# Combine turns of a two-layer token tower: vector operations of different rows laced, and head outputs in two row blocks in place of three

## The chip, the cores and the metric

The kernel runs on one core of a Trainium2 chip, in float32. The metric is the device time of one execution in microseconds (us). The kernel before was timed three times; its median is 1458.46 us.

A core has TensorE (PE in the profile; its weight loads are PEld), VectorE (DVE), ScalarE (ACT), GpSimd (POOL) and SyncE (SP, which here only issues transfers). Each engine takes its own instructions in the order in which they are written. Between engines, and between two instructions of one engine where one needs what the other writes, order is kept by semaphores.

## The reference, cut to what matters

The tower embeds 32 batches of 128 tokens with 192 features and runs two layers. Layer 0 is causal attention and a soft mixture of 64 experts. Layer 1 is attention with 12 heads of 16 features and a router that sends each token to one of 8 experts. The change lies in the stretch from the end of layer 0's experts up to layer 1's router:

```python
Y = einsum('bsd,bms->bmd', Ys, C)            # combine: softmax weights times slot outputs
h = h + Y
x = layernorm(h);  q, k, v = x @ w_qkv.T     # 12 heads of 16
q = rope(q * scale);  k = rope(k)
attn = softmax(q @ k.T)                      # per head, 128 x 128
h = h + (attn @ v) @ w_proj.T + b_proj
x = layernorm(h);  logits = x @ router_w
expert = argmax(logits)                      # row of the token: count of earlier tokens of this expert
```

## The kernel before, in words

`tower_program` has four phases one behind the other: `tower_phase` (embedding, attention 0, slot inputs), `expert_phase` for 64 experts, `combine_phase`, and `expert_phase` for 8 experts. Everything changed is in `combine_phase` and in the host layout of one weight.

`combine_phase` works on one batch of 128 tokens after the other, in 38 turns (t = 0 to 37). A turn works at up to eight stages of different batches at once. The letters of `turn(t, u, n, y, q, a, p, r, z, w)` name the batch that a stage handles: n (t+1) subtracts the maximum from the combine logits (`less_max`) and exponentiates them; y (t) makes Y = C·Ys, adds it to h, and normalises it to `x4`; q (t-1) makes q, k, v, rotates q and k, and transposes them; a (t-2) makes scores, softmax and head outputs; p (t-3) projects the heads and adds to h, and normalises it to `x5`. Of router pairs of two batches, r (odd turns from 5 on) makes logits, z (even turns from 6 on) chooses experts and counts, and w (odd turns from 7 on) works out the rows and scatters the tokens.

Each engine has a `turn` of its own in which the stages' operations are written out by hand in one order; that order is the schedule. The order of PE in a turn is: Y (8 matmuls), q and k (5), the projection (3), the router's transposes (r) or the counts (z), transposes of the probabilities (12), of q and k (6), router (r), of x4 (2), v (5), scores (12), transposes of the inverse sums (3), head outputs (12).

On DVE a turn begins with two reductions (L1709) that give the maximum of each head's scores; ACT then makes the exponentials (L1601), and PE's counts, router transposes and transposes of the probabilities wait for them. DVE goes on with `place` (w) or `choose` (z), `oT`, `less_max`, the addition of Y, the statistics of layer norm 4 (L1730 to L1733), the rotation (L1744 to L1753, ending in `qk_padded`), `x4` (L1759, L1760), statistics of layer norm 5 and the inverse sums. A dependent operation waits for a count in the semaphore `steps` (`st.link`, `st.wait`). At the end it waits for ACT's `x4T_hi` (L1628), which can start once v is made, and writes `x4T_lo` (L1781), `x4T_hi_over_lo` (L1783) and `x5` (L1789).

POOL makes both reciprocal square roots of a turn (L1428). In turns with w they are queued behind two indirect transfers that scatter the tokens (L1437), which wait for `to_i` (L1702).

The head outputs come out transposed. With 4 heads on 32 partitions each (16 in use), 12 heads take three row blocks of 128 columns, `bank[32*s:32*s+32, 1, g*P:(g+1)*P]` for head 4g+s. `oT` is these times the inverse sums; the sums are widened to 3×128 columns (L1774), transposed by PE (L1570) and copied by ACT (L1634). The projection adds three products with `Wproj_padded`, whose spare rows are zero but for the one of the bias.

## Time and profile before

| | us |
|---|---|
| runs shown | 1458.09, 1458.46, 1460.61 |
| median | 1458.46 |
| the profiled execution's own time | 1450.89 |
| its span in the profile | 1449.2 |

The profiled execution is 7.6 us shorter than the median of the runs shown. Times of single operations are read from it. Its mean granted TensorE clock is 0.979 of full speed. The combine turns run from about 914 us to about 1294 us of the span.

How to read it: a row of the timeline gives start, duration, engine, line, operation, written tile <- read tiles, shapes and count, and in brackets the idle time of the engine before it with what ended it. L60 is the helper `matmuls`, so its rows are told apart by their tiles. Durations of neighbouring DVE rows overlap by some 0.08 us where the second does not wait for the first.

### The profile page before, as it was taken

How to read it: one execution, taken by the hardware profiler on the slowest of the kernel's cores; microseconds unless marked ns; L12 is line 12 of the kernel's file. 1: busy time of each engine (PE TensorE's matmuls, PEld its weight loads, DVE VectorE, ACT ScalarE, POOL GpSimd, SP SyncE). 2: the span in 40 equal slices, each digit the busy share in tenths (PEclk: the TensorE clock that was granted, in tenths of full speed). 3: DMA queues.
4: the chain of work that ended last, by engine and by line, in shares of the span. 5: the costliest groups of instructions: out<-in, count | busy, mean ns of one | idle time of the engine just before them, and what ended most of it. 6: DMA issues, size and time to landing. Idle time of an engine off the chain costs nothing. (4 is left out here: it accounts for less than half of the span.)

```text
span 1449.2 us, 29984 instructions
## 1 busy us (share of the span) xinstructions
PE 1364.3 (94%) x9221; PEld 1214.8 (84%) x9221; DVE 1002.1 (69%) x2920; ACT 940.8 (65%) x2207; POOL 261.1 (18%) x284
## 2 busy tenths in 40 slices
PE   6899999988899999999999999799999999869995
PEld 4678888877799989999899998689999899758885
DVE  7787777543777777777777774489989899832321
ACT  1378888876566666666666664288888888725551
POOL 6231100000111111111111110102122122121344
PEclk8899999999999999999999999999999999979998
DMA  7036666567466666666666665545445447116641
GB/s 214 20 110 161 161 150 150 150 165 193 141 184 198 188 192 196 183 198 188 192 196 183 198 188 167 159 139 155 133 154 153 130 146 198 42 41 148 145 79 19
DMA packets 202709, 221.17 MB, mean 153 GB/s; under 512 B 30068, under 2 KB 169402, under 8 KB 202608
## 3 DMA queue, kind: packets, MB, share of 16 engines
q1 hardware_dynamic: 170032, 180.15, 44.9%
q10 hardware_dynamic: 24896, 32.80, 6.7%
q0 software_dynamic: 7680, 6.95, 2.6%
q8 instruction: 54, 0.88, 0.3%
q14 instruction: 47, 0.39, 0.1%
HBM read 142.46 MB, written 79.90 MB: 153 GB/s over the span
## 5 line engine op out<-in xcount | busy, mean ns | idle before, releaser
L1116 PE MATMUL bank<-e_w,e_h_full 128*128 128x192 f32 x1920 | 324.5, 326 | 0.3
L1116 PEld LDWEIGHTS bank<-e_w,e_h_full 128*128 128x128 f32 x1920 | 310.6, 190 | 1.2 <-ACT e_h_full L1187 0.8
L1187 ACT ACTIVATE e_h_full<-bank,e_b 128x512 f32<-128x512 f32 x240 | 165.1, 688 | 193.6 <-PE bank L60 193.6
L1053 POOL TENSOR_TENSOR e_ln_rstd<-e_ln_var_eps,minus_half 128x4 f32<-128x4 f32 x64 | 64.8, 1013 | 515.1 <-DVE e_ln_var_eps L1238 515.1
L1601 ACT ACTIVATE probs<-bank,head_neg_max 128x128 f32<-128x128 f32 x384 | 134.5, 392 | 2.5 <-DVE head_neg_max L1709 1.2
L1245 DVE TENSOR_SCALAR e_rows<-e_slot_sums,e_ln_mean_var,e_ln_rstd 128x192 f32<-128x192 f32 x256 | 80.0, 377 | 76.2 <-POOL e_ln_rstd L1053 76.2
L1157 ACT ACTIVATE e_x_full<-bank,e_ln_shift,e_ln_gain 128x512 f32<-128x512 f32 x128 | 92.5, 773 | 48.7 <-PE bank L1089 44.9
L885 PE MATMUL bank<-x,dispatch_weights 128*128 128x193 f32 x512 | 95.8, 330 | 11.0 <-ACT slot_stage L739 10.4
L60 PE MATMUL bank<-e_x_hi,e_w1hi 128*128 128x512 f32 x216 | 95.6, 443 | 4.6 <-DVE e_w1lo L1224 3.0
L621 DVE TENSOR_REDUCE column_neg_max<-bank 128x4 f32<-128x512 f32 x64 | 44.2, 690 | 80.5 <-PE bank L60 80.3
L1483 PE MATMUL bank<-slot_outputs_then_w_part,combineT 128*128 128x193 f32 x512 | 94.2, 337 | 2.7 <-ACT combineT L1593 2.1
L1270 DVE TENSOR_TENSOR e_stage<-bank,e_b 128x768 f32<-128x768 f32 x64 | 61.3, 958 | 48.3 <-PE bank L1116 48.3
L885 PEld LDWEIGHTS bank<-x,dispatch_weights 128*128 128x128 f32 x512 | 82.1, 190 | 14.3 <-issue 14.3
L1483 PEld LDWEIGHTS bank<-slot_outputs_then_w_part,combineT 128*128 128x128 f32 x512 | 84.7, 192 | 9.2 <-issue 9.2
L1601 ACT ACTIVATION_READ_ACCUMULATOR probs<-bank,head_neg_max 128x1 f32 x384 | 89.1, 232 | 0.0
L60 PE MATMUL bank<-e_x_hi,e_w1lo 128*128 128x512 f32 x216 | 85.3, 395 | 0.0
L60 PE MATMUL bank<-e_x_lo,e_w1hi 128*128 128x512 f32 x216 | 85.2, 394 | 0.0
L60 PE MATMUL bank<-e_x_hi_over_lo,e_w1hi 128*128 128x512 f32 x216 | 84.9, 393 | 0.0
L60 PE MATMUL bank<-e_x_hi_over_lo,e_w1lo 128*128 128x512 f32 x216 | 84.6, 392 | 0.0
L67 PE MATMUL bank<-spare_operand 128*128 128x512 f32 x253 | 69.0, 421 | 14.2 <-PEq L1383 8.6
L719 ACT ACTIVATE slot_exp<-bank,column_neg_max 128x128 f32<-128x128 f32 x256 | 72.8, 374 | 14.6 <-DVE column_neg_max L621 14.6
L1163 ACT ACTIVATE e_x_hi<-e_x_full 128x1024 fp32r<-128x1024 f32 x72 | 76.2, 1058 | 7.6
(255 smaller groups left out, 3138.1 us busy)
## 6 DMA issues: line engine op xcount, KB each, us to landing
slot_sums<-slot_stage SPq DMA_DIRECT2D x64, 386.0 KB
e_slot_sums<-slot_sums SPq DMA_DIRECT2D x64, 386.0 KB, 3.6
slot_outputs<-e_stage ACTq DMA_DIRECT2D x64, 384.0 KB, 3.3
slot_outputs_then_w_part<-slot_outputs SPq DMA_DIRECT2D x32, 768.0 KB, 4.9
e_w<-in_w SPq DMA_DIRECT2D x64, 288.0 KB, 2.9
slot_logits<-kept_logits SPq DMA_DIRECT2D x64, 256.0 KB, 3.3
slot_logits<-slot_logits SPq DMA_DIRECT2D x32, 512.0 KB, 3.4
e_w1raw<-in_w SPq DMA_DIRECT2D x80, 192.0 KB, 2.8
```

Source lines behind the costliest of these rows:

```text
L60: last = pe.matmul(out, w, m, start=n == 0, stop=n == len(pairs) - 1, **kw)
L67: pe.matmul(out, T["spare"][:, 0:P], T["spare"][:], start=True, stop=True)
L719: last = act.activation(ls[:, n % 2, js], logits_bank(n)[:, js], ACT.Exp, bias=nmc[:, n % 2, j:j + 1])
L885: last = pe.matmul(U[:, j // 2, j % 2, :], disp[:, n % 2, j * P:(j + 1) * P], x3[n // NC % 3][:, j, 0:1 + D], start=True, stop=True)
L1053: pool.tensor_tensor(rs[u][:], ve[u][:], half[:], ALU.pow).then_inc(rstd_ready, 1)
L1116: last = pe.matmul(ybank(u)[:, j // 2, (j % 2) * D:(j % 2 + 1) * D], hf[:, k, js], w2s[u][:, k, :], start=k == 0, stop=k == MT - 1)
L1157: last = act.activation(xf[:, k, :], bank[:, k, :], ACT.Identity, bias=lnb[:, k, ds(n, 1)], scale=lng[:, k, ds(n, 1)])
L1163: act.activation(xhi[u][:], xf[:], ACT.Copy).then_inc(x_hi_ready, 1)
L1187: act.activation(hf[:, m, :], hbank(u, m), act_fn, bias=b1s[:, m, ds(n, 1)]).then_inc(acted, 1)
L1245: last = dve.tensor_scalar(rows[u][:, j, 0:D], sums[u][:, j, 1:], mv[u][:, j, 0:1], rs[u][:, j:j + 1], ALU.subtract, ALU.mult)
L1483: last = pe.matmul(bank[:, 0, 0:D + 1], cT[:, c, :], ysb[u][:, c, :], start=c == 0, stop=c == NC - 1)
L1601: last = act.activation(pr[:, s, g, :], bank[:, 4 + s, g * P:(g + 1) * P], ACT.Exp, bias=nmx[:, s, g:g + 1], accum_out=esum[:, s, g:g + 1])
```

## The change

It has two parts.

**Head outputs.** Heads 2k and 2k+1 of the first eight share the 32 partitions of group k: v is stored by head with 32 columns, an even head's 16 features in the first half and an odd head's in the second half, the other half zero. Two products into the same partitions and columns are added up. The first eight heads thus fill one row block, and the last four take a second one. There are still 12 head matmuls. The transposes of the inverse sums go from 3 to 2, the projection's products from 3 to 2, `oT` and `einvT` from 384 to 256 columns. The sums are widened in two copies of 128 columns in place of one of 384. The bias row moves to row 16 of the second part.

**Order on DVE.** `choose` and `place` are dissolved, and their dependent operations, those of the layer norms and the reciprocals are written between operations of other stages. The waits remain, but for a count noted by `mark` when the earlier operation was issued. The diff, cut to its core:

```diff
+    def mark(self, ins):
+        self.did(ins)
+        return self.base + self.n
...
-        einv_wide, oT = sb("head_inv_wide", [P, 3, 4, 2 * HD]), sb("oT", [P, 3 * P])
-        einvT = sb("head_invT", [P, 3 * P])
+        einv_wide, oT = sb("head_inv_wide", [P, 2, P]), sb("oT", [P, 2 * P])
+        einvT = sb("head_invT", [P, 2 * P])
...
-                        matmuls(pe, projected, [(oT[:, g * P:(g + 1) * P], Wp[:, g, :]) for g in range(3)]
+                        matmuls(pe, projected, [(oT[:, g * P:(g + 1) * P], Wp[:, g, :]) for g in range(2)]
...
-                        for g in range(3):
-                            for s in range(4):
-                                last = pe.matmul(bank[32 * s:32 * s + 32, 1, g * P:(g + 1) * P], vs[u][:, 4 * g + s, :],
-                                                 pT[:, s, g, :], start=True, stop=True)
+                        for first, step, rows, start, stop in ((0, 2, 0, True, False), (1, 2, 0, False, True),
+                                                               (8, 1, 1, True, True)):
+                            for k in range(4):
+                                head = first + step * k
+                                last = pe.matmul(bank[32 * k:32 * k + 32, 1, rows * P:(rows + 1) * P], vs[u][:, head, :],
+                                                 pT[:, head % 4, head // 4, :], start=start, stop=stop)
...
-                        act.activation(vs[1 - u][:, :, 0:HD], bank[:, 3, 0:D].rearrange("p (a d) -> p a d", d=HD),
+                        by_halves = vs[1 - u][:].rearrange("p (i b) (e d) -> p i (b e) d", b=2, e=2)
+                        act.activation(by_halves[:, :, 0:4:3, :],
...
                     if w is not None:
-                        place(w)
+                        part = st.mark(dve.tensor_reduce(lsum[:], lex[:], AX_X, ALU.add))
...
                     if n is not None:
                         less_max(n)
+                    if w is not None:
+                        st.wait()
+                        dve.tensor_copy(to_i[w % 3][:], row_f[:]).then_inc(S["placed"], 1)
...
                         st.did(dve.tensor_tensor(straight[:], src, cos[:], ALU.mult))
+                    if y is not None:
+                        wait_apart(dve, S["h2_ready"], y + 1)
+                        stats4 = st.mark(dve.bn_stats(st6[:, 0, :], h[:, y, :]))
...
+                    if a is not None:
+                        dve.wait_ge(S["S_exp"], 4 * a + 4)
+                        inverse = st.mark(dve.reciprocal(einv[:], esum[:]))
+                    if p is not None:
+                        wait_apart(dve, S["h3_ready"], p + 1)
+                        stats5 = st.mark(dve.bn_stats(st6[:, 1, :], h[:, p, :]))
                     if y is not None:
                         dve.wait_ge(S["ln4_rstd"], y + 1)
```

What this makes of the order is seen in three places. The first is DVE in an odd turn with w, from the operation behind the two reductions to the first one of the rotation. `to_i` is the row number that starts POOL's scatter, `row_inv` and `h_all` add Y, and BN_STATS and BN_AGGR are layer norm 4. Before:

```order
L1695 TENSOR_TENSOR row_by_expert<-row_by_expert,onehot 128x16
L1697 TENSOR_REDUCE router_sum<-router_exp 128x2
L1699 TENSOR_REDUCE row_of_token<-row_by_expert 128x2
L1700 RECIPROCAL x_rows<-router_sum 128x2
L1702 CAST to_i<-row_of_token 128x2
L1721 TENSOR_TENSOR oT<-bank,head_invT 128x384
L1660 TENSOR_TENSOR slot_logits<-slot_logits,token_neg_max_rows 128x1024
L1726 RECIPROCAL row_inv<-bank 128x1
L1727 SCALAR_TENSOR_TENSOR h_all<-bank,row_inv,h_all 128x192
L1730 BN_STATS ln_stats<-h_all 128x6
L1732 BN_AGGR ln_mean_var<-ln_stats 128x2
L1733 TENSOR_SCALAR ln_var_eps<-ln_mean_var 128x1
```

After:

```order
L1705 TENSOR_TENSOR row_by_expert<-row_by_expert,onehot 128x16
L1707 TENSOR_REDUCE router_sum<-router_exp 128x2
L1717 TENSOR_TENSOR oT<-bank,head_invT 128x256
L1720 TENSOR_REDUCE row_of_token<-row_by_expert 128x2
L1721 RECIPROCAL x_rows<-router_sum 128x2
L1666 TENSOR_TENSOR slot_logits<-slot_logits,token_neg_max_rows 128x1024
L1729 CAST to_i<-row_of_token 128x2
L1736 RECIPROCAL row_inv<-bank 128x1
L1743 SCALAR_TENSOR_TENSOR h_all<-bank,row_inv,h_all 128x192
L1755 TENSOR_TENSOR rope_straight<-bank,rope_cos 128x384
L1758 BN_STATS ln_stats<-h_all 128x6
L1760 TENSOR_TENSOR rope_crossed<-bank,rope_sin 128x192
```

`oT` and `less_max` (L1666) now stand ahead of the cast `to_i`, and the statistics of layer norm 4 stand inside the rotation.

The second place is DVE in the same turn, from `qk_padded`, for which PE's transposes of q and k wait, to the router's maximum. The tile x is `x4`, for which PE's two transposes ahead of v wait. Before:

```order
L1753 TENSOR_TENSOR qk_padded<-rope_straight,rope_crossed 128x24x16
L1759 TENSOR_SCALAR x<-h_all,ln_mean_var,ln_rstd 128x192
L1760 TENSOR_SCALAR x<-h_all,ln_mean_var,ln_rstd 128x64
L1766 BN_STATS ln_stats<-h_all 128x6
L1768 BN_AGGR ln_mean_var<-ln_stats 128x2
L1769 TENSOR_SCALAR ln_var_eps<-ln_mean_var 128x1
L1773 RECIPROCAL head_inv<-head_exp_sum 128x12
L1774 COPY head_inv_wide<-head_inv 128x384
```

After:

```order
L1775 TENSOR_TENSOR qk_padded<-rope_straight,rope_crossed 128x24x16
L1780 RECIPROCAL head_inv<-head_exp_sum 128x12
L1783 BN_STATS ln_stats<-h_all 128x6
L1787 TENSOR_SCALAR x<-h_all,ln_mean_var,ln_rstd 128x192
L1788 TENSOR_SCALAR x<-h_all,ln_mean_var,ln_rstd 128x64
L1792 BN_AGGR ln_mean_var<-ln_stats 128x2
L1688 COPY head_inv_wide<-head_inv 128x128
L1691 COPY head_inv_wide<-head_inv 128x128
L1799 TENSOR_SCALAR ln_var_eps<-ln_mean_var 128x1
```

A reciprocal and the statistics of layer norm 5 now stand between `qk_padded` and `x4`.

The third place is PE, from the transposes of the inverse sums of one turn into the next. Before:

```order
L1570 MATMUL bank<-ident,head_inv_wide 128x128 x3
L1581 MATMUL bank<-probsT,v_padded 32x128 x12
L1483 MATMUL bank<-e_slot_outputs_then_w_part,combineT 128x193 x8
L60 MATMUL bank<-Wqkv_hi,x4T_hi 128x384
L60 MATMUL bank<-Wqkv_lo,x4T_hi 128x384
L60 MATMUL bank<-Wqkv_hi,x4T_lo 128x384
L60 MATMUL bank<-Wqkv_hi,x4T_hi_over_lo 128x384
L60 MATMUL bank<-Wqkv_lo,x4T_hi_over_lo 128x384
L60 MATMUL bank<-Wproj_padded,oT 128x192 x3
```

After:

```order
L1574 MATMUL bank<-ident,head_inv_wide 128x128 x2
L1586 MATMUL bank<-probsT,v_by_head 32x128 x12
L1487 MATMUL bank<-e_slot_outputs_then_w_part,combineT 128x193 x8
L60 MATMUL bank<-Wqkv_hi,x4T_hi 128x384
L60 MATMUL bank<-Wqkv_lo,x4T_hi 128x384
L60 MATMUL bank<-Wqkv_hi,x4T_lo 128x384
L60 MATMUL bank<-Wqkv_hi,x4T_hi_over_lo 128x384
L60 MATMUL bank<-Wqkv_lo,x4T_hi_over_lo 128x384
L60 MATMUL bank<-Wproj_two_parts,oT 128x192 x2
```

Nothing moved on PE; one transpose and one product of the projection are gone from each turn.

## Rows read from the trace of the kernel before

**Rows 1.** Windows: busy us of each engine, granted clock, DMA, in 22 turns

```profile
963.74:1201.00 237.26, 234.96 (x2448) 215.77 (x2450) 214.59 (x678) 197.80 (x726) 52.88 (x75) 1.00 0.48 145
```

**Rows 2.** Timeline: the first DVE reduction of turns 5, 21, 22, 23 and 32

```profile
963.55 0.95 DVE L1709 TENSOR_REDUCE head_neg_max<-bank 128x6 f32<-128x768 f32 x1
...
1136.32 0.95 DVE L1709 TENSOR_REDUCE head_neg_max<-bank 128x6 f32<-128x768 f32 x1
...
1147.44 1.81 DVE L1709 TENSOR_REDUCE head_neg_max<-bank 128x6 f32<-128x768 f32 x2
...
1157.79 1.81 DVE L1709 TENSOR_REDUCE head_neg_max<-bank 128x6 f32<-128x768 f32 x2
...
1254.71 0.95 DVE L1709 TENSOR_REDUCE head_neg_max<-bank 128x6 f32<-128x768 f32 x1
```

**Rows 3.** Timeline of even turn 22: PE, ACT and DVE behind the exponentials

```profile
1152.77 0.30 PEld L60 LDWEIGHTS bank<-onehot,upto 128*128 128x128 f32 x2
...
1154.82 0.64 PEld L1528 LDWEIGHTS bank<-ident,qk_padded 128*128 128x128 f32 x6 [0.27 <-DVE qk_padded L1753]
...
1155.43 0.25 PEld L1546 LDWEIGHTS bank<-ident,x 128*128 128x128 f32 x2
...
1156.55 0.38 ACT L1628 ACTIVATE x4T_hi<-bank 128x256 fp32r<-128x256 f32 x1
...
1157.05 0.28 DVE L1781 TENSOR_TENSOR x4T_lo<-bank,x4T_hi 128x128 fp32r<-128x128 f32 x1
```

**Rows 4.** Timeline of odd turn 21: PE and ACT behind the exponentials

```profile
1141.66 0.42 PEld L1505 LDWEIGHTS bank<-ident,x_rows 128*128 128x128 f32 x4
...
1143.65 0.64 PEld L1528 LDWEIGHTS bank<-ident,qk_padded 128*128 128x128 f32 x6 [0.26 <-DVE qk_padded L1753]
...
1145.15 0.25 PEld L1546 LDWEIGHTS bank<-ident,x 128*128 128x128 f32 x2
...
1146.27 0.38 ACT L1628 ACTIVATE x4T_hi<-bank 128x256 fp32r<-128x256 f32 x1 [0.90 <-PE bank L60]
```

**Rows 5.** Timeline of turn 21: small DVE operations, the last one waiting for `row_of_token`

```profile
1138.33 0.17 DVE L1699 TENSOR_REDUCE row_of_token<-row_by_expert 128x2 f32<-128x16 f32 x1
...
1138.42 0.15 DVE L1700 RECIPROCAL x_rows<-router_sum 128x2 f32<-128x2 f32 x1
...
1138.61 0.17 DVE L1702 CAST to_i<-row_of_token 128x2 int32<-128x2 f32 x1
```

**Rows 6.** Timeline of turn 22: head matmuls, last product of q and k, DVE's rotation

```profile
1147.46 0.59 PEld L1581 LDWEIGHTS bank<-probsT,v_padded 128*32 128x32 f32 x24 [0.17 <-issue]
...
1151.69 0.34 PE L60 MATMUL bank<-Wqkv_lo,x4T_hi_over_lo 128*128 128x384 f32 x1
...
1152.21 0.36 DVE L1730 BATCH_NORM_STATS2 ln_stats<-h_all 128x6 f32<-128x192 f32 x1
...
1152.97 0.55 DVE L1744 TENSOR_TENSOR rope_straight<-bank,rope_cos 128x384 f32<-128x384 f32 x1
...
1154.22 0.55 DVE L1753 TENSOR_TENSOR qk_padded<-rope_straight,rope_crossed 128x384 f32<-128x384 f32 x1
...
1154.98 0.31 DVE L1760 TENSOR_SCALAR x<-h_all,ln_mean_var,ln_rstd 128x64 f32<-128x64 f32 x1
```

**Rows 7.** Timeline of turn 21: DVE's `less_max`, POOL's scatter; last the scatter of turn 31

```profile
1139.19 1.22 DVE L1660 TENSOR_TENSOR slot_logits<-slot_logits,token_neg_max_rows 128x1024 f32<-128x1024 f32 x1
...
1139.58 1.74 POOL L1437 DMA_INDIRECT routed_inputs<-x_rows,to_i  x1 [3.93 <-DVE to_i L1702]
...
1141.62 0.98 POOL L1437 DMA_INDIRECT routed_inputs<-x_rows,to_i  x1 [0.30 <-issue]
...
1142.61 0.59 POOL L1428 TENSOR_TENSOR ln_rstd<-ln_var_eps,minus_half 128x1 f32<-128x1 f32 x1
...
1246.93 1.04 POOL L1437 DMA_INDIRECT routed_inputs<-x_rows,to_i  x1 [3.90 <-DVE to_i L1702]
```

**Rows 8.** Groups by line: loads of the projection's weights, 6 in each of 32 turns

```profile
L60 PEld LDWEIGHTS bank<-Wproj_padded,oT 128*128 128x128 f32 x192 | 32.3, 189 | 3.7 <-DVE oT L1721 3.6
```

More of the change, by code:

```diff
@@ L246, in __init__ @@
         self.C_ready, self.C_exp = sem("C_ready"), sem("C_exp")
[L247 removed]
+        self.Wp = sb("Wproj_two_parts", [P, 2, D])
     def load_logits(self, sp, b):
@@ L1568, in turn @@
                         pe.wait_ge(S["einv_ready"], a + 1)
[L1569 to L1571 removed]
+                        for g in range(2):
+                            last = pe.transpose(bank[:, 2, g * P:(g + 1) * P], einv_wide[:, g, :], ident[:])
                         last.then_inc(S["einvT_done"], 1)
@@ L1750, in turn @@
                     if q is not None:
-                        st.wait()
+                        dve.wait_ge(steps, turned)
                         past(dve, S["qkT_done"], q)
@@ L1838, in host_layout, with projection_parts @@
     }
-def padded_projection(w, b):
-    t = np.zeros((4, 2 * HD, 3, D), np.float32)
-    t[:, 0:HD] = w.reshape(3, 4, HD, D).transpose(1, 2, 0, 3)
-    t[0, HD, 0] = b
-    return t.reshape(P, 3, D)
+def projection_parts(w, b):
+    t = np.zeros((2, P, D), np.float32)
+    t[0] = w[0:P]
+    for k in range(4):
+        first = 2 * HD * k + HD * (k % 2)
+        t[1, first:first + HD] = w[P + HD * k:P + HD * (k + 1)]
+    t[1, HD] = b
+    return np.ascontiguousarray(t.transpose(1, 0, 2))
 def rope_tables():
```

104 lines of the change are left out of this document (55 added, 49 removed).

## The prediction

> **What bounds the kernel now.** I read four views. The windows come first, for whether one engine is simply full. In 22 turns of 237.26 us PE is busy for 234.96, DVE for 214.59 and ACT for 197.80, at full clock (2.4 GHz, granted 1.00) [rows 1]. That looks like PE, but a matmul's row runs on while it waits in the pipe, so the second view is the start of each turn. The two reductions of DVE begin at 1136.32, 1147.44 and 1157.79: 11.12 us for an odd turn, 10.35 for an even one; from turn 5 to turn 32 it is 291.16 us for 14 odd and 13 even turns [rows 2]. 14 × 11.12 + 13 × 10.35 is 290.2; 0.9 us are small irregular pauses.
>
> The third view, the timeline, shows a ring through three engines that closes once a turn. I count from the start R of the reductions. ACT turns the maxima into 12 exponentials, and PE may go on with counts or router transposes at R + 5.33 (even, 1152.77) or R + 5.34 (odd, 1141.66) [rows 2 to 4]. PE then transposes the probabilities and reaches the transposes of q and k, where it waits 0.27 and 0.26 us for DVE's `qk_padded` [rows 3, 4]. Behind it come the transposes of x4, v, ACT's `x4T_hi` (1.12 us behind the first x4 transpose in both turns), DVE's `x4T_lo` and, two operations on, the next R: 0.74 us from 1157.05 to 1157.79 [rows 2 to 4]. So the reader is to see a ring with one stall in it of some 0.27 us a turn, and in the even turn another 0.08, since `x4T_lo` starts 0.12 behind the end of `x4T_hi` (1156.93) where 0.04 is a release.
>
> **The change part by part.**
>
> *Less work on PE.* A weight load of the projection takes 0.168 us per issue (32.3 us / 192), and two of the six of a turn go: 0.33 us [rows 8]. A transpose is about 0.12 us (two x4 transposes, 0.25) [rows 3]: 0.12 us for the one that goes. But both lie ahead of the point at which PE waits for the exponentials, and the projection is no part of the ring. PE merely comes to that point 0.45 us sooner and waits. Worth to the ring: nothing directly. The transpose lets everything from the head outputs to the product of q and k start 0.12 us sooner.
>
> *Head matmuls.* They stay 12. Before, 24 loads take from 1147.46 to about 1148.2, and the row says 0.59 [rows 6]. The new thing is that four of them add to what the four before have written. The trace has no such pair in this size; bounds are 0 and, if the second four waited until the first four are through, about a third of 0.59 for a pause, 0.2 us. I take 0, since each product here is already two passes into one place (24 loads for 12 products).
>
> *Less copying.* `oT` and the transposed sums have 256 columns in place of 384. On DVE 384 columns take 0.55 us and 192 features 0.36 [rows 6], so 128 columns less are some 0.13 us. The widening becomes two copies of 128, about as long together as the one, and it has cover: what waits for it is PE's third-to-last step of the turn. ACT's shorter copy has cover too.
>
> *Lacing.* The row of small operations gives its price: an operation that needn't wait starts 0.09 us behind the other (1138.33 to 1138.42), one that waits for it 0.19 (to 1138.61) [rows 5]. So a link costs 0.1. From R to the rotation's first operation it is 5.53 us now (1152.97) [rows 2, 6]. The statistics that move behind that operation are 0.76 of it (1152.21 to 1152.97) [rows 6], links 0.3, `oT` 0.13: DVE could start at R + 4.3. But the rotation reads PE's product of q and k, whose last matmul ends at 1152.03, R + 4.59 [rows 6]; 0.12 sooner and with a release of 0.05 it is R + 4.52. PE ends last there now. From the rotation's start to `qk_padded` it is 1.25 us now (to 1154.22) [rows 6], and with the statistics in it (0.36, then two small ones, each less the overlap of 0.08) 0.48 more. So `qk_padded` starts at R + 6.25 in place of R + 6.78, and is through for PE at R + 6.85. PE is there at 1154.55, R + 7.11 [rows 3]. **The stall goes**, with 0.26 us to spare. In odd turns the product comes up to 0.2 later after R, and PE reaches the place at R + 7.07: it goes too, with little to spare.
>
> *What is late next, even turns.* The operations on x4 now stand behind a reciprocal and BN_STATS. Now the second ends at 1155.29, 1.07 us behind the start of `qk_padded` [rows 6]; added are 0.15 for the reciprocal [rows 5] and 0.28 for the statistics (0.36 less 0.08) [rows 6], and 0.04 for the release: PE may start its x4 transposes at R + 6.25 + 1.54 = R + 7.79. Without any stall it would be there at 1155.43 − 0.27, R + 7.72; now it is there at R + 7.99 [rows 2, 3]. The ring gains 0.20 of the 0.27, and DVE is no longer late for `x4T_lo`, since the widening stands further ahead: 0.08. **Even: 0.27 us** (between 0.1 and 0.35).
>
> *What is late next, odd turns.* The router's matmuls stand between, so PE comes to the x4 transposes at 1145.15 − 0.26, R + 8.57 [rows 2, 4]; DVE alone would be ready by R + 8. But x4 needs the reciprocal square root that POOL makes behind the two scatter transfers [rows 7]. They wait for the cast `to_i`, at R + 2.29 now [rows 2, 5]. It moves behind `oT` and `less_max` (start to start some 0.34 + 1.13) less 0.2 for links: R + 3.55, 1.25 later. The first transfer thus starts at R + 4.5 (1139.58 + 1.25). How long is it? 1.74 us where `less_max` runs beside it, 1.04 where it doesn't [rows 7]; after the change `less_max` is over by then. I take 1.04, then the pause of 0.30, 0.98 for the second, up to 0.46 more since `qk_padded` (also two operands in SBUF) now runs beside it, and 0.59 for the square root: R + 7.9. Then the two operations on x4 and releases, 0.65: R + 8.55. PE would be there at R + 8.57. So it just fits. **Odd: 0.26 us**; if the transfer stays 1.74 it is nothing (below).
>
> The Trainium skill, page "SBUF — State Buffer", section "SBUF: two separate sides", says that a Vector operation with two SBUF inputs and a GpSimd operation that reads SBUF share a port pair that one of them holds for its whole instruction. The trace agrees in that the transfer is 0.70 us longer beside `less_max` [rows 7]; by the rule the moved transfer would be the short one.
>
> *Placements without cost.* `chosen` and the counts come later, with PE's wait for the exponentials as cover. SP's queue isn't touched; the projection's weight is a third smaller and is loaded long before. ACT's order is unchanged.
>
> **The sum.** 14 × 0.26 + 13 × 0.27 = 7.2 us. The turns before 5 and after 31 have the same steps with less to hide them; the last batch's own chain loses 0.33 + 0.12 once, and two full turns without router may gain 0.1 each: 0.6. Together 7.8 us. Against the profiled execution's 1450.89 that is 1443.1; that execution was 7.6 us below the median of the runs shown, and I carry the difference over: 1458.5 − 7.8 = 1450.7 us. The irregular 0.9 us I leave; with the stall gone some may be hidden.
>
> **The rivals.**
>
> *The scatter stays long.* If the first transfer takes 1.74 at its new place, the square root is there at R + 4.5 + 1.74 + 0.30 + 0.98 + 0.59 = R + 8.1 or more and x4 at R + 8.8. That is where PE starts today (1145.15, R + 8.83): the 13 odd turns with a scatter gain nothing, 3.4 us less, 1454.1. For it: the new place has other DVE operations beside it, `qk_padded` and the statistics among them; against it: the 1.04 of turn 31.
>
> *Links cost nothing.* If laced operations don't start sooner, only `oT`'s 0.13 is left. `qk_padded` comes 0.13 sooner, odd turns gain 0.13, and in even turns x4 is through at R + 6.65 + 1.54 = R + 8.19, 0.20 later than now, less the 0.08: 14 × 0.13 − 13 × 0.12 is 0.3; with the 0.6 it is some 1457.6. Against it are the 0.09 and 0.19 [rows 5].
>
> The Trainium skill, page "VectorE: DVE Perf Modes", section "The DRAIN you can't avoid", says just this: that a semaphore between two operations costs nothing extra, since the next one waits for an empty pipe anyway. By it the change would give the time of this rival; the rows above disagree with it for small operations.
>
> *Slower: the odd turn hangs on POOL.* If both transfers take 1.74 at the new place, the square root is ready at R + 4.5 + 1.74 + 0.30 + 1.74 + 0.59 = R + 8.9 and x4 at R + 9.55, 0.72 later than now. 13 × 0.72 is 9.4 us lost, less 3.5 of the even turns and 0.8 of the rest: about 5 us slower, 1463.6. It decides from the point at which the square root comes later than R + 8.2. For it: the cast is moved 1.25 us, and nothing on POOL was taken away. Against: the second transfer, beside the rotation, takes 0.98 today.
>
> *Slower: added-up head outputs pause.* 0.2 us ahead of Y and of q and k in each turn; `qk_padded` is then through at R + 7.05 in even turns (no stall) but x4 at R + 7.99, and in odd turns a stall of 0.15 returns: only some 3 us are left of the gain, 1455.5. This is the near end of that unknown; it takes a pause above 0.4 to be slower.
>
> *More than that.* If DVE is quicker than I counted, even turns save 0.35, and the pauses of 0.9 are covered: 9.9 us, 1448.6. More is not to be had, since the ring without stalls is R + 10.86 and R + 10.0, whatever DVE does.
>
> **How the numbers follow.** Forecast, with the better case, 0.55. Scatter long or a pause in the head outputs, still faster: 0.21. Links cost nothing: 0.10. Slower by POOL, or by something of its kind: 0.14. The predicted time is 1450.7 us. The range runs from 1447 (more than the better case by the spread of the runs, 1.5 us) to 1458 (the case without gain); left out are the slower case and a little below. 0.2% of the time, 2.9 us, is about what a measurement of this kernel can tell from no change. Faster by more is the first two, 0.76; within is the third, 0.10; slower is the last, 0.14.
>
> **What the profile after would show.** No idle time of PE ahead of the transposes of q and k, and instead idle time ahead of the counts and router transposes, ended by ACT's exponentials, of some 0.5 us a turn. R to R of 10.86 and 10.08 us. In even turns at most 0.1 us ahead of the x4 transposes, ended by DVE's x4. The first scatter of a pair at R + 4.5 with 1.04 us. PE's busy share falls although the time does. Wrong would be: idle time ahead of the x4 transposes of odd turns ended by DVE, with POOL's square root behind R + 8.2 (the scatter), a start of the rotation behind R + 4.7 (head outputs or DVE), or a turn that shortens by more than 0.35 us, which would mean that the exponentials' part of the ring isn't fixed.

## The result, and the profile after

The changed kernel takes 1447.94 us, the median of six runs (1443.63 to 1450.16). The kernel before takes 1457.32 us beside it, also of six (1452.49 to 1460.61). The ratio is 0.9944, with a 95% interval of 0.9921 to 0.9966: faster, by 3.4 to 7.9 parts in a thousand. Timed again later (experiment 11) the ratio was 0.9956 [0.9937, 0.9975]. The forecast was 1450.7 us.

The profiled execution of the changed kernel took 1449.45 us, with a span of 1447.7. That is only 1.4 us less than the profiled one of before, although the medians lie 9.4 apart. Where the turns run, the gain is seen in full. These are the same stages as in [rows 1], 22 turns, in the windows' view (us, then busy us of PE, PE's loads, DVE, ACT and POOL, the granted clock, DMA share, GB/s):

```profile
969.05:1199.40 230.35, 225.95 (x2380) 205.67 (x2371) 193.04 (x700) 193.13 (x726) 46.09 (x75) 1.00 0.49 150
```

The start R of DVE's reductions in turns 5, 21, 22, 23 and 32 of the changed kernel (timeline: start, duration; compare [rows 2]):

```profile
968.86 0.95 DVE L1699 TENSOR_REDUCE head_neg_max<-bank 128x6 f32<-128x768 f32 x1
...
1136.53 1.82 DVE L1699 TENSOR_REDUCE head_neg_max<-bank 128x6 f32<-128x768 f32 x2
...
1147.40 1.81 DVE L1699 TENSOR_REDUCE head_neg_max<-bank 128x6 f32<-128x768 f32 x2
...
1157.43 1.82 DVE L1699 TENSOR_REDUCE head_neg_max<-bank 128x6 f32<-128x768 f32 x2
...
1251.90 0.95 DVE L1699 TENSOR_REDUCE head_neg_max<-bank 128x6 f32<-128x768 f32 x1
```

The 27 full turns from 5 to 32 take 283.04 us, where they took 291.16 [rows 2]: 8.12 less. An odd turn takes 10.87, an even one 10.03 us.

The two spans are balanced by four stretches. (1) The first reduction of turn 2 stands at 933.62 before and at 939.37 after. The phases ahead of it, which the change doesn't touch, took 5.75 us more in this execution:

```profile
939.37 1.81 DVE L1699 TENSOR_REDUCE head_neg_max<-bank 128x6 f32<-128x768 f32 x2
```

(2) Turns 2 to 4 take 0.44 us less. (3) The 27 full turns take 8.12 less. (4) From turn 32 on, the last rows up to the end of the last scatter take 39.44 in place of 38.48 us, 0.96 more, and what is behind them 0.39 more. 5.75 − 0.44 − 8.12 + 0.96 + 0.39 = −1.46, the difference of the spans. In the twelve other profiled executions of this study the same point came between 937.5 and 944.7 us; the one of before is the early one.

How the ring looks now is seen in even turn 22, R = 1147.40 (timeline of the changed kernel; the brackets give the idle time ahead and what ended it, and are printed from 0.15 us on):

```profile
1151.90 0.56 DVE L1755 TENSOR_TENSOR rope_straight<-bank,rope_cos 128x384 f32<-128x384 f32 x1 [0.25 <-PE bank L60]
...
1152.73 0.30 PEld L60 LDWEIGHTS bank<-onehot,upto 128*128 128x128 f32 x2 [0.51 <-ACT probs L1606]
...
1153.56 0.55 DVE L1775 TENSOR_TENSOR qk_padded<-rope_straight,rope_crossed 128x384 f32<-128x384 f32 x1
...
1154.48 0.69 PEld L1532 LDWEIGHTS bank<-ident,qk_padded 128*128 128x128 f32 x6
...
1154.65 0.31 DVE L1788 TENSOR_SCALAR x<-h_all,ln_mean_var,ln_rstd 128x64 f32<-128x64 f32 x1
...
1155.14 0.25 PEld L1550 LDWEIGHTS bank<-ident,x 128*128 128x128 f32 x2
```

The stall of [rows 3] ahead of the transposes of q and k is gone: no bracket at 1154.48. None stands ahead of the x4 transposes (1155.14) either. PE's pause has moved ahead of the counts, 0.51 us, and it is ACT's last exponential that ends it. The odd turn 21, R = 1136.53, with POOL:

```profile
1138.42 0.42 DVE L1717 TENSOR_TENSOR oT<-bank,head_invT 128x256 f32<-128x256 f32 x1
...
1138.90 1.21 DVE L1666 TENSOR_TENSOR slot_logits<-slot_logits,token_neg_max_rows 128x1024 f32<-128x1024 f32 x1
...
1140.99 1.04 POOL L1441 DMA_INDIRECT routed_inputs<-x_rows,to_i  x1 [6.04 <-DVE to_i L1729]
...
1141.86 0.42 PEld L1509 LDWEIGHTS bank<-ident,x_rows 128*128 128x128 f32 x4 [0.28 <-ACT probs L1606]
...
1142.33 0.98 POOL L1441 DMA_INDIRECT routed_inputs<-x_rows,to_i  x1 [0.30 <-issue]
...
1142.92 0.55 DVE L1775 TENSOR_TENSOR qk_padded<-rope_straight,rope_crossed 128x384 f32<-128x384 f32 x1
1143.32 0.59 POOL L1432 TENSOR_TENSOR ln_rstd<-ln_var_eps,minus_half 128x1 f32<-128x1 f32 x1
...
1144.23 0.31 DVE L1788 TENSOR_SCALAR x<-h_all,ln_mean_var,ln_rstd 128x64 f32<-128x64 f32 x1
...
1145.11 0.25 PEld L1550 LDWEIGHTS bank<-ident,x 128*128 128x128 f32 x2
```

The first scatter is 1.04 us long in place of 1.74 [rows 7], and x4 is there at 1144.54, 0.57 us before PE takes it. The waits of 24 turns say the same (engine and line, for whom it waited, us in total, times, longest):

```profile
PEld bank L60 <- ACT probs L1606: 6.3, 12, 0.8
...
PEld bank L1509 <- ACT probs L1606: 3.2, 11, 0.3
```

These two are the waits for the exponentials in even and in odd turns. Before, the same view of the same stretch has 14 waits of PE for `qk_padded`, 11 of them in even turns and three in odd ones (9, 15 and 21), and hardly one for ACT's exponentials:

```profile
PEld bank L1528 <- DVE qk_padded L1753: 3.6, 14, 0.3
...
PEld bank L60 <- ACT probs L1601: 0.3, 1, 0.3
...
PEld bank L1505 <- ACT probs L1601: 0.2, 1, 0.2
```

### The profile page after: what moved, and what is told of

It is laid out like the page before. It is cut to its first block and busy times, and to the rows that moved or that the text cites. A ratio compares the mean times of both kernels' runs of the same rounds, so it can differ in the third digit from the quotient of the medians.

```text
span 1447.7 us, 29824 instructions
## 1 busy us (share of the span) xinstructions
PE 1357.5 (94%) x9125; PEld 1204.7 (83%) x9125; DVE 972.3 (67%) x2952; ACT 935.1 (65%) x2207; POOL 253.5 (18%) x284
```

## The experiments

Twelve kernels were run. The table gives, from the profiled execution of each, the 27 full turns, the median odd and even turn, the time from R of turn 32 to the end of the last scatter ("drain"), and the span; then the time, and the ratio to the kernel before on the same chip where it was timed in rounds.

| | 27 turns | odd | even | drain | span | time (median) | ratio |
|---|---|---|---|---|---|---|---|
| before | 291.16 | 11.12 | 10.35 | 38.48 | 1449.2 | 1457.32 | 1 |
| changed | 283.04 | 10.87 | 10.03 | 39.44 | 1447.7 | 1447.94 | 0.9944 |
| 1 heads only | 286.37 | 10.99 | 10.15 | 39.48 | 1454.5 | 1455.24 | 0.9978 [0.9964, 0.9992] |
| 2 lacing only | 285.82 | 11.08 | 10.04 | 37.47 | 1447.6 | 1448.10 | 0.9922 [0.9901, 0.9942] |
| 3 statistics only | 286.34 | 11.08 | 10.05 | 36.45 | 1445.0 | 1451.56 | 0.9968 [0.9942, 0.9994] |
| 4 idle products | 283.39 | 10.88 | 10.04 | 35.03 | 1440.9 | 1444.00 | 0.9913 [0.9886, 0.9940] |
| 5 POOL later | 288.80 | 11.31 | 10.04 | 37.46 | 1452.7 | 1454.38 | one run |
| 6 cast early | 283.44 | 10.88 | 10.05 | 39.24 | 1448.8 | 1450.48 | one run |
| 7 eleven exps | 276.87 | 10.60 | 9.87 | 38.40 | 1443.7 | 1445.41 | one run |
| 8 the same, x4 first | 279.26 | 10.85 | 9.78 | 34.35 | 1439.7 | 1441.38 | one run |
| 9 heads, statistics, idle | 283.43 | 10.88 | 10.05 | 38.74 | 1444.8 | 1444.79 | 0.9937 [0.9914, 0.9959] |
| 10 x4 first, idle | 283.05 | 10.87 | 10.03 | 35.01 | 1440.6 | 1445.57 | 0.9949 [0.9931, 0.9968] |
| 11 changed again | 283.44 | 10.88 | 10.05 | 39.27 | 1448.0 | 1449.20 | 0.9956 [0.9937, 0.9975] |
| 12 lacing, two products | 283.15 | 10.89 | 10.03 | 39.42 | 1453.3 | 1455.02 | one run |

The kernel before took 1458.62 us as a median beside 1 to 4, 1456.78 (one run) beside 5 to 8, 1454.43 beside 9 to 11, and 1463.85 (one run) beside 12. The medians of 2 and 4 rest on four runs each. The turns repeat to 0.4 us (the changed kernel: 283.04 and 283.44). The whole time does not, so causes are read from the turns.

**Experiments 1 to 3: the parts alone.** The first keeps the head outputs in two row blocks and takes DVE's order back to that of before (`choose` and `place` in one piece, statistics of layer norm 4 behind Y). The second keeps DVE's new order and takes the heads back to three row blocks. The third has, of the whole change, this and nothing else:

```diff
-                        wait_apart(dve, S["h2_ready"], y + 1)
-                        st.did(dve.bn_stats(st6[:, 0, :], h[:, y, :]))
-                        st.wait_apart()
-                        st.link(dve.bn_aggr(mv[:, 0, :], st6[:, 0, :]))
-                        dve.tensor_scalar(ve[:, 0:1], mv[:, 0, 1:2], EPS, None, ALU.add).then_inc(S["ln4_var"], 1)
...
+                    if y is not None:
+                        wait_apart(dve, S["h2_ready"], y + 1)
+                        stats4 = st.mark(dve.bn_stats(st6[:, 0, :], h[:, y, :]))
...
+                    if y is not None:
+                        wait_apart(dve, steps, stats4)
+                        stats4 = st.mark(dve.bn_aggr(mv[:, 0, :], st6[:, 0, :]))
```

Expected of the first:

> The kernel before with the new head layout alone, DVE's order as before. Theory (a ring of DVE, ACT and PE with one stall ahead of the transposes of q and k): only oT's 0.13 us lies between the start R of the reductions and qk_padded, so 0.13 of the stall of 0.27 goes; R to R 10.99 in odd and 10.22 in even turns, about 3.5 us of the 8 in the 27 full turns. Rival (PE's work is what bounds): 0.45 us a turn gone from PE shortens each turn by 0.45, 12 us in all.

Expected of the second:

> The changed kernel with three row blocks of head outputs as before, DVE's new order kept. Theory: the rotation waits for PE's product of q and k, 0.12 us later than in the changed kernel, and qk_padded is still in time: odd 10.87, even 10.10 to 10.15 (x4 some 0.1 later), so all but 1 to 2 us of the changed kernel's gain. Rival (links cost nothing): as the kernel before, 11.12 and 10.35.

Expected of the third:

> The kernel before with one thing moved: the three statistics operations of layer norm 4 stand between those of the rotation. Theory: 0.76 us leave the way to the rotation and 0.48 come back inside it, which is what the stall of 0.27 needs: odd 10.86, even 10.0 (x4 isn't behind anything new), thus as much as the whole change or 1 us more. Rival (the sum of all lacing is needed): half of it or less, odd above 10.95 and even above 10.15.

Measured: the heads alone take 4.79 us off the 27 turns, the lacing alone 5.34, the move of the statistics alone 4.82. All three expectations missed: some 3.5, 6.1 to 7.1 and 8 or more were expected. Together the two parts give 8.12, less than their sum, since both remove the same stall. Of the lacing, the statistics are nearly all: the dissolved `choose` and `place` and the reciprocals add 0.5 us in 27 turns. The even turn is at 10.04 as soon as the statistics stand inside the rotation. The odd turn is not: 11.08 with either form of the lacing, 10.87 only with the heads too. The timeline of an odd turn of experiment 2, R = 1137.61, shows why:

```profile
1142.06 1.01 PEld L60 LDWEIGHTS bank<-Wproj_padded,oT 128*128 128x128 f32 x6
...
1143.04 0.52 PEld L1509 LDWEIGHTS bank<-ident,x_rows 128*128 128x128 f32 x4
...
1143.53 1.34 PEld L1524 LDWEIGHTS bank<-ident,probs 128*128 128x128 f32 x12
...
1144.84 0.69 PEld L1532 LDWEIGHTS bank<-ident,qk_padded 128*128 128x128 f32 x6
```

No row has a bracket. PE goes from the projection straight into the router's transposes, at R + 5.43, when the last exponential is through at R + 5.3. Its transposes of the probabilities start at R + 5.92; in the changed kernel it is 1142.25, R + 5.72. Half of these 0.20 us is that PE comes later; the other half is that four transposes without a pause ahead of them take 0.49 us up to the next row's start, and 0.39 behind a pause (1141.86 to 1142.25). PE comes too late for the odd turn here, and the 0.33 us of the projection count. Experiment 12 tests that.

**Experiment 12: the projection alone.** Experiment 2 with one edit; the last four heads are left out of the projection.

```diff
-                        matmuls(pe, projected, [(oT[:, g * P:(g + 1) * P], Wp[:, g, :]) for g in range(3)]
+                        matmuls(pe, projected, [(oT[:, g * P:(g + 1) * P], Wp[:, g, :]) for g in range(2)]
```

> All of DVE's new order, head outputs in three row blocks as before, but the projection adds only the first two of its three products, so the last four heads are left out of it (their outputs are still made, copied and transposed). Nothing else differs from the kernel with the lacing alone, which had odd turns of 11.08 and even turns of 10.04 us. Theory: in its odd turns PE has no pause from Y to v, and the six loads of the projection keep it beyond the last exponential; without two of them (0.33 us) PE is at the router's transposes at R + 5.33 instead of R + 5.43, waits there some 0.25 us for the exponentials, and odd turns take 10.87 to 10.90 us, even turns 10.04. The 27 turns take 283.0 to 283.6 us. Rival: it is the missing transpose and the shorter oT (128 columns) that shorten the odd turn, by letting Y and the product of q and k start sooner; then odd turns stay at 11.0 to 11.08 us and the 27 turns at 285 to 286 us.

Measured: 283.15 us, odd turns 10.89, even 10.03, as the theory says. The transposes and `oT` are as large as before in this kernel, so the 2.7 us to experiment 2 come from the projection's two loads. In its odd turn with R = 1142.05:

```profile
1146.52 0.69 PEld L60 LDWEIGHTS bank<-Wproj_padded,oT 128*128 128x128 f32 x4
...
1147.39 0.42 PEld L1509 LDWEIGHTS bank<-ident,x_rows 128*128 128x128 f32 x4 [0.17 <-ACT probs L1605]
```

PE is at the router's transposes at R + 5.34 and waits for ACT again.

**Experiment 5: where POOL decides.** Two idle operations of POOL, of the kind of the square root, are queued between the scatters and the square root of turns with w:

```diff
+                    if w is not None:
+                        for j in range(2):
+                            pool.tensor_tensor(idle[:, j:j + 1], rank[:, j:j + 1], half[:, 0:1], ALU.pow)
```

> The changed kernel with two small POOL operations (a power of one column each, on a spare tile) between the two scatter transfers and the reciprocal square roots, in the 13 turns with a scatter. Theory: each takes 0.55 us as the square root does, so the root for x4 ends at R + 8.5 in place of R + 7.4, x4 is ready at R + 9.15 and PE, which now starts its x4 transposes at R + 8.58, waits for it: odd turns 11.4 in place of 10.87, about 7 us in all, even turns unchanged. Rival (POOL has more slack than I counted): odd turns stay below 11.0.

Measured: odd turns 11.31 us, 0.44 more, and 5.8 us in the 27 turns where 7 were expected; even turns unchanged. The timeline of the odd turn with R = 1141.24:

```profile
1145.69 1.04 POOL L1442 DMA_INDIRECT routed_inputs<-x_rows,to_i  x1 [6.04 <-DVE to_i L1733]
1147.03 0.97 POOL L1442 DMA_INDIRECT routed_inputs<-x_rows,to_i  x1 [0.30 <-issue]
1148.02 1.09 POOL L1448 TENSOR_TENSOR idle<-rank,minus_half 128x1 f32<-128x1 f32 x2
1149.08 0.53 POOL L1433 TENSOR_TENSOR ln_rstd<-ln_var_eps,minus_half 128x1 f32<-128x1 f32 x1
...
1150.31 0.20 PEld L1554 LDWEIGHTS bank<-ident,x 128*128 128x128 f32 x2 [0.40 <-DVE x L1792]
```

The square root is ready at 1149.61, R + 8.37, and PE waits 0.40 us for x4. In the changed kernel it is ready at R + 7.38. By these rows an odd turn can't hide a square root that comes later than about R + 7.95 (an estimate: 8.37 less the 0.40 to 0.44).

**Experiment 6: the cast ahead of `less_max`.** `to_i` stands just ahead of `less_max`, so that the first scatter runs beside it again.

```diff
-                    if n is not None:
-                        less_max(n)
                     if w is not None:
                         st.wait()
                         dve.tensor_copy(to_i[w % 3][:], row_f[:]).then_inc(S["placed"], 1)
+                    if n is not None:
+                        less_max(n)
```

> The changed kernel with the cast to_i ahead of less_max instead of behind it. Theory: the first scatter transfer starts about a microsecond sooner and runs beside less_max again, so it takes 1.4 to 1.75 us in place of 1.04, and no turn changes: odd 10.87, even 10.03. Rival (the length of the transfer has to do with the turn and not with less_max): it stays 1.04.

Measured (turn with w near 1140 us):

```profile
1140.37 1.22 DVE L1666 TENSOR_TENSOR slot_logits<-slot_logits,token_neg_max_rows 128x1024 f32<-128x1024 f32 x1
...
1141.27 1.24 POOL L1441 DMA_INDIRECT routed_inputs<-x_rows,to_i  x1 [5.06 <-DVE to_i L1727]
```

The scatter overlaps the last 0.32 us of `less_max` and takes 1.24 us, less than expected, since the transfer starts 0.80 us behind the end of the cast (1140.47). In [rows 7] the scatter starts 0.39 us into `less_max`, overlaps 0.83 us of it and takes 1.74. In experiment 9 the overlap is 0.70 us and the scatter takes 1.61; with no overlap it is 1.04. So its length follows the overlap. The turns don't move (283.44), so the short scatter is worth nothing by itself: experiment 9, with its 1.61, has the same odd turn of 10.88.

**Experiments 7 and 8: is it the exponentials that end last?** The seventh leaves out one of ACT's twelve exponentials in each turn (head 0's probabilities then stay those of the first turn):

```diff
-                            for g in range(3):
+                            for g in range(1 if s == 0 and a > 0 else 0, 3):
```

> The changed kernel without the exponentials of head 0 (from the second batch of turns on; the old values are used, so head 0 of the output is left out of the right computation). ACT's part of the ring is 0.34 us shorter. Theory: the other parts are nearly as long: in even turns x4 is ready at R + 7.74 whatever ACT does, so they stay at 10.0; in odd turns the projection is through at R + 5.05 and qk_padded at R + 6.98, so 10.8. Rival (the exponentials are the one bound): every turn 0.34 us shorter, 10.53 and 9.69.

Measured: odd turns 10.60, even 9.87, that is 0.27 and 0.16 less, where 10.8 and 10.0 were expected. So the ring does run through ACT; but only half of the 0.34 arrives in even turns, because x4 ends last next. The waits of 24 turns have a new row:

```profile
PEld bank L1550 <- DVE x L1788: 2.4, 12, 0.2
...
PEld bank L60 <- ACT probs L1606: 1.9, 12, 0.2
```

The eighth adds that in even turns the two operations on x4 stand ahead of the reciprocal and of BN_STATS of layer norm 5:

```diff
+                    if y is not None and w is None:
+                        dve.wait_ge(S["ln4_rstd"], y + 1)
+                        past(dve, S["x4T_done"], y)
+                        dve.tensor_scalar(x4[:, 0:D], h[:, y, :], mv[:, 0, 0:1], rs[:, 0:1], ALU.subtract, ALU.mult)
```

> The run before (head 0 left out of the exponentials, thus of the right computation) with the two x4 operations directly behind qk_padded in turns without a scatter, as in the kernel before. Theory: x4 is ready at R + 7.27 in even turns and no longer bounds them: even 9.7 to 9.8, odd as in the run before. Rival (something else holds the even turns): even 10.0 as before.

Measured: even turns 9.78, as expected, and the wait for x4 is gone. But odd turns took 10.85, so an odd and an even turn together take 20.63 us, 0.16 more than in experiment 7. In its place PE waits longer ahead of the scores of even turns. The row of PE's loads names ACT's copy of q and k, the row of its matmuls a read of DVE:

```profile
PEld bank L1566 <- ACT headsT_kq L1628: 5.4, 12, 0.5
...
PE bank L1566 <- DVE row_by_expert L1683: 3.7, 12, 0.3
```

It is the second that ends last. `row_by_expert` reads the counts out of a bank that the scores write, and in this kernel it stands behind x4, the reciprocal and the statistics: it ends at R + 8.59 in place of R + 8.33 in experiment 7 (medians of the even turns), while ACT's copy ends at R + 8.52 and R + 8.51. The scores start at R + 8.73, 0.17 later, and the next R comes 0.09 sooner. So in the odd turn PE stands 0.26 later after R (Y at R + 0.99 in place of R + 0.73), comes to the router's transposes at R + 5.09 without a pause in place of R + 4.98 behind one, and takes 0.10 more for them, as in experiment 2. That is 0.21 of the 0.25 us that the odd turn gives back.

**Experiment 4: the last rows.** Behind turn 32 PE has little to do, and its clock falls. This is the window of turn 32 in the changed kernel and in experiment 4 (columns as above; the granted clock is the third number from the end):

```profile
1256.00:1261.00 5.00, 3.77 (x19) 3.77 (x20) 2.03 (x11) 2.72 (x12) 0.68 (x2) 0.66 0.06 20
```

```profile
1256.00:1261.00 5.00, 4.64 (x70) 4.18 (x73) 2.00 (x10) 2.70 (x6) 0.68 (x2) 1.00 0.00 0
```

The changed kernel's mean of 0.66 is made of both levels, 2.4 and 1.2 GHz; in experiment 4 all of it is at 2.4. What PE did before, in the changed kernel:

```profile
1257.23 0.30 PEld L60 LDWEIGHTS bank<-onehot,upto 128*128 128x128 f32 x2 [2.42 <-ACT probs L1606]
...
1257.74 2.58 PEld L1524 LDWEIGHTS bank<-ident,probs 128*128 128x128 f32 x12
```

It was idle for 2.42 us ahead of the counts, and the twelve transposes of the probabilities behind them take 2.58 us where they take 1.34 in a full turn. Experiment 4 fills the idle time with products that nobody reads:

```diff
+                    if t in (NB, NB + 1):
+                        pe.wait_ge(S["v_took"], t - 1)
+                        keep_busy(pe, T, bank[:, 3, :], 10 if t == NB else 8)
```

> The changed kernel with 10 and 8 idle products on spare operands behind the projection in turns 32 and 33, where PE waits for the exponentials. Theory: in the changed kernel PE is idle for 2.4 us there in turn 32 and the granted clock falls to half, so that the transposes of the probabilities take 2.58 us in place of 1.34; with the products the clock stays, R of turn 32 to R of turn 33 is 10.0 in place of 11.65, and turn 33 gains about 2 us too: 3 to 4 us in all. Rival: the clock falls all the same and nothing is gained, or PE comes late.

Measured in experiment 4:

```profile
1253.24 2.20 PEld L67 LDWEIGHTS bank<-spare_operand 128*128 128x128 f32 x10
...
1255.70 0.30 PEld L60 LDWEIGHTS bank<-onehot,upto 128*128 128x128 f32 x2 [0.26 <-ACT probs L1609]
...
1256.14 1.34 PEld L1527 LDWEIGHTS bank<-ident,probs 128*128 128x128 f32 x12
```

The drain takes 35.03 in place of 39.44 us. Whether the change makes this dip more likely is open. Of the profiled kernels without idle products, those before the change and in experiments 2 and 3, which have the longer projection and idle times of 1.3 to 2.0 us here, have no dip in turn 32. The changed kernel and experiments 1, 6, 7, 11 and 12 have it, behind 1.79 to 2.43 us of idle time. But experiment 5 has 2.43 us and no dip, and experiment 8 has 2.08 and none. So the idle time alone does not decide. With the idle products of experiments 4, 9 and 10 it did not fall in turn 32. Experiment 5, which has no dip there, has a drain of 37.46 us, 1.0 less than the kernel before.

**Experiments 9 to 11: which parts are needed.** The ninth has the new heads, of the lacing the statistics alone, and the idle products. The tenth is experiment 4 with x4 first in even turns, as in experiment 8. The eleventh is the changed kernel.

> The head outputs in two row blocks, of DVE's new order only the statistics of layer norm 4 inside the rotation, and 10 and 8 idle products of PE behind the projection of turns 32 and 33. Choose and place stay as they were, and with them the scatter's first transfer beside less_max (1.74 us). Theory: the rest of the lacing is worth 0.5 us or less, since the statistics alone gave 286.3 us for the 27 full turns against 285.8 with all of the lacing; so here the turns take 283.0 to 283.9 us (odd 10.87, even 10.04), the drain of the last rows 35, and the whole is within 1 us of the changed kernel with idle products (1440.9 in the profiled execution, 1444.0 as a median). Rival: with the projection shorter DVE's small operations are what ends last, and the links count: the turns take 284.5 us or more, and the kernel is 1.5 us or more behind.

> The changed kernel with the two operations on x4 ahead of the reciprocal and the statistics of layer norm 5, in even turns alone, and the idle products of turns 32 and 33. Theory: PE doesn't wait ahead of the x4 transposes of even turns in the changed kernel, so x4 comes sooner for nothing: turns 283.0 to 283.6 us, even 10.03, the whole within 0.5 us of the changed kernel with idle products. Rival: x4 comes so late in the changed kernel that it is late now and then; then even turns take 9.95 to 10.0 and the 27 turns 282.0 to 282.7 us.

> The changed kernel once more, on the same chip as the two above. Its ratio to the kernel before was 0.9944 in six runs. Expected: 0.993 to 0.997, with 283 us for the 27 full turns. The dip of TensorE's clock in turn 32 is there or not, since the kernels without a shorter projection had it or not at equal idle time: 12 x 1.34 us or 12 x 2.5 us for the products of the projection, q and k behind the idle time, and a drain of 39.4 or some 37.5 us.

Measured: the turns are 283.43, 283.05 and 283.44 us. So the rest of the lacing is worth nothing that can be seen in the turns once the heads are in two row blocks, and x4 first is worth nothing either. The drain is 35.01 in the tenth, and 39.27 in the eleventh with the dip in turn 32. In the ninth it is 38.74, against the expectation: the dip came a turn later. There `choose` and `place` stand ahead of `oT` again, and the projection of turn 33 waits longer for `oT`:

```profile
1264.50 1.14 PEld L60 LDWEIGHTS bank<-Wproj_two_parts,oT 128*128 128x128 f32 x4 [2.12 <-DVE oT L1730]
1265.62 3.21 PEld L67 LDWEIGHTS bank<-spare_operand 128*128 128x128 f32 x8
```

In experiment 4 the same row has 1.60 us of idle time, and eight products behind it take 1.75 us; here they take 3.21, at half the clock. As medians the ninth and the tenth are 4.4 and 3.6 us below the changed kernel on the same chip, but the intervals overlap, and single runs spread over 10 to 15 us. The tenth's drain shows where some 4 us come from; that it is a gain in the median is likely, not settled.

## Why the prediction was right, point by point

The forecast was 7.8 us, 7.2 of it in the full turns. The full turns gave 8.1. The sign, the size and the place are right, and in even turns the mechanism too. In odd turns the size is in part luck: one step was wrong and cost nothing here, because the two parts of the change came together.

*The ring.* Right. PE goes on at R + 5.33 in both turns (1152.73 and 1141.86), as forecast from [rows 2 to 4]. R to R is 10.87 and 10.03 us, against 10.86 and 10.08. PE's pause for the exponentials, forecast at some 0.5 us a turn, is 0.51 in even turns but 0.28 in odd ones, where PE comes later after R than I took it to. Experiment 7 shows that ACT's exponentials are in it.

*"Less work on PE … worth to the ring: nothing directly."* This is the step that failed. I said that both savings lie "ahead of the point at which PE waits for the exponentials". In [rows 3] PE waited there for 0.06 us, in [rows 4] for 0.13, and turn 21 is not like most odd turns: it follows an even turn of 10.55 us, 0.20 longer than the others, so PE had come early. The odd turn 23 of the kernel before, R = 1157.79, is like nine of the 14:

```profile
1163.17 0.52 PEld L1505 LDWEIGHTS bank<-ident,x_rows 128*128 128x128 f32 x4
1163.66 1.34 PEld L1520 LDWEIGHTS bank<-ident,probs 128*128 128x128 f32 x12
1165.12 0.64 PEld L1528 LDWEIGHTS bank<-ident,qk_padded 128*128 128x128 f32 x6
```

PE comes out of the projection at R + 5.38 and doesn't wait for the exponentials at all, and the stall ahead of `qk_padded` is 0.12 us (1165.00 to 1165.12), not 0.26. PE's work already counted in odd turns. So the 0.26 forecast for an odd turn came out, 0.25, but from two sources: PE is at the transposes of the probabilities 0.14 sooner after R (R + 5.72 in place of 5.86, medians), which is the shorter work on PE, and the rest, some 0.11, is the stall. Take away the stall alone, and the odd turn stays at 11.08 (experiment 2); two loads of the projection, 0.33 us, bring it to 10.89 (experiment 12). These two loads are 2.7 of the 8.1 us. For the lacing alone I had 6.1 to 7.1 us, and it gave 5.34.

What was missing is PE's way from one place where it waits for the exponentials to the next. In experiment 2 it leads from the counts of even turn 22 (R + 5.34) to the router's transposes of turn 23 (R + 5.44) and takes 10.14 us; its one wait on another engine is 0.31 us for ACT's copy of q and k. In the changed kernel the exponentials free PE every 10.03 us in this place. PE's loads without their waits are not more than the ring: an odd and an even turn of experiment 2 take 21.12 us, and less the 0.31 and 0.08 us in which PE waits it is 20.73, where I took 20.86 for the ring. It is the way with ACT's copy in it that is longer.

*Head matmuls.* Right: 24 loads in 0.59 us, and the next step of PE starts 0.79 us behind their start, where it was 0.80. Adding up two products in one place costs no pause.

*Less copying.* Right: `oT` takes 0.42 us, where 0.55 less 0.13 was forecast.

*The rotation and the stall.* Right to 0.1 us. The rotation starts at R + 4.50 in turn 22, bound by PE (forecast 4.52), `qk_padded` at R + 6.16 (forecast 6.25), and the stall is gone in both turns.

*The links.* The price was read rightly, but it is paid where it doesn't count. Small operations that needn't wait start 0.07 to 0.09 us apart in the changed kernel, less than the 0.19 of a link [rows 5]. But the rotation waits 0.25 us for PE's product, so that the three links saved ahead of it are only waiting time (experiment 3 against 2, and 9 against 11). It was the statistics, 0.76 us, that had to go. The Trainium skill's sentence on a semaphore between two operations (page "VectorE: DVE Perf Modes", section "The DRAIN you can't avoid") does not fit these rows. The rival's time, 1457.6 us, fell, but that says nothing about links: it left out that moving the statistics helps even if links are free, and experiment 3, with hardly another link dissolved, takes 4.82 us off the turns.

*x4, even turns.* Right: PE starts its transposes at R + 7.74 (forecast 7.79) without waiting, and half of experiment 7's gain stops there. The 0.27 forecast became 0.32, and its bound was 0.35.

*x4, odd turns.* Right in its result, too dark in one term. The first scatter starts at R + 4.46 (forecast 4.5) and takes 1.04. The second was to take up to 0.46 more beside `qk_padded`; it takes 0.98. So the square root is there at R + 7.38, not at 7.9, and x4 at R + 8.01 for a PE that comes at R + 8.58. "It just fits" was a slack of 0.57 us. By the rule of the Trainium skill (page "SBUF — State Buffer", section "SBUF: two separate sides"), of a DVE operation with both inputs in SBUF and a POOL operation that reads SBUF, the one that starts first has the shared ports for its whole instruction, and the other waits. The lengths of the scatters agree: `less_max` starts ahead of the scatter of [rows 7] and stretches it, `qk_padded` starts 0.59 us into the second scatter and leaves it at 0.98. The forecast had not asked which of the two starts first. That `qk_padded` would be held off in turn is not seen: it takes its 0.55 us as before.

*The rivals.* The long scatter didn't come. The slower case by POOL is a real mechanism, as experiment 5 shows, with a point of decision nearer to R + 7.95 than to the R + 8.2 that I gave; the change stays 0.57 us on the good side of it. The pause in the head outputs didn't come.

*The drain.* Forecast was a gain of 0.6 with turns 2 to 4. They gave 0.44, and the last rows lost 0.96 in the profiled execution by the dip of the clock. I had not looked at the clock there, though it falls in the kernel before too, in turn 33.

*The median.* I carried over the 7.6 us by which the profiled execution of before lay under its runs. That was right: up to the first reduction of turn 2 it was 4 to 11 us shorter than all the other profiled executions. 9.4 us by the first set of runs and 5.2 by the second lie on both sides of 7.8.

## What to carry to other kernels

Before a stall is called the only slack of a ring, look at more than one turn, and at the place where the engine is believed to wait: a row without idle time ahead of it means that the engine's own way up to there is about as long as the ring. Follow that way from one such wait to the next, across the turn's end and with the waits that will stay. When a chain on one engine waits for another's product, move operations behind that wait; taking out small waits ahead of it was worth 0.5 us at most here. Where TensorE goes idle for long near the end, look at its granted clock: half the clock for the next operations can cost more than a change to the main loop brings.

## What the runs showed of the hardware

The time of an execution goes with its mean granted TensorE clock. Over 47 runs of the kernel before, each 0.001 less of mean clock goes with 1.5 us more; their clocks lie between 0.976 and 0.986. The ten runs of experiment 1 lie between 0.971 and 0.977. That goes with a median only 3.4 us below the kernel before, although its turns are 4.8 us shorter; that the lower clock is the cause is likely, not shown. Why its clock is lower is open: in its profile the dips lie in the phases ahead of the turns too, which it shares with all the others.

An idle time of 2.1 to 2.4 us of PE is followed by half the clock in some executions and not in others, of kernels with the same instructions there. A scatter of POOL takes 1.04, 1.24, 1.61 or 1.74 us when it overlaps 0, 0.32, 0.70 or 0.83 us of an addition of two 128x1024 tiles in SBUF that started ahead of it. An addition of 384 columns that starts within it doesn't stretch it.
